# Cross-attention head: where two output chunks and the second group's query chunks are split

## The chip, the cores and the metric

One Trainium2 chip, one core of it. The metric is the device time of one execution in microseconds (us), the median of several runs. Engines are named as the profile names them: PE is TensorE's matmul stream, PEld its weight loads, DVE is VectorE, ACT is ScalarE, POOL is GpSimd, SP is SyncE, which here issues the loads.

## What is computed

Two layers over x (16 sequences of 64 tokens, 512 features: 1024 token rows, 8 tiles of 128): a windowed attention, a gated feed-forward part, a cross-attention and a routed feed-forward part, each on a layer-normed x and each added back to x. The change touches the third:

```
q = (layernorm(x) @ Wq) in 32 heads of 128;  k, v = (ctx @ Wk), (ctx @ Wv) in 8 heads of 128
q, k = rotary(q), rotary(k)
scores = q k^T / sqrt(128), masked;  attn = softmax(scores)
x = x + (attn v) @ Wo
```

Four query heads share one key and value head, so the work falls into 8 groups; a group has 512 columns of Wq, 128 of Wk, 128 of Wv and 512 rows of Wo.

## The kernel before

Every float32 product is made of three matmuls (`mm3`, lines 121 to 123): each operand is split into a high part and a low part. A weight chunk of 128 x 512 is split by two engines: ACT copies the loaded chunk `raw` to the high part (line 1354, `high`), and POOL subtracts it from the chunk, which gives the low part (line 1507, `low`). `W` is a ring that holds both parts.

Cross-attention is a software pipeline of 64 units: unit n treats token tile n % 8 of group n // 8. Each engine has a function `step(n, u, g)`, and its instructions run strictly in the order written there. The first eight units are written out with n a plain number (`past` is false), the later ones stand in a loop. In step n

- PE makes keys and values of unit n (`KV`, weights `ca_wkv`), then the queries of two heads (`QT`, weights `W`, operand `NTh`/`NTl`) as soon as `rope_read` of the unit before is given, transposes K (line 1293), transposes the token tiles that are due (line 233), then does the scores of unit n - 2 (line 1309), the transposes of the probabilities of unit n - 3 (line 1319), the output product of unit n - 4 (`O`) and the value product of unit n - 3 (line 1343).
- DVE, where tiles are due, counts them (line 198), aggregates (208), adds epsilon (210), and normalises (222, `X` to `qT`); then row sums and reciprocals of unit n - 3, the rotary products of unit n (line 1474), then cap and row maxima of unit n - 2 (1490, 1495), and last the low part of the transposed tiles (245).
- POOL raises the variance of the due tiles to the power -1/2 (line 216, `root`, the operand that `normalise` waits for), scales the probabilities of unit n - 3 (line 1534), makes low parts of weights (line 1507), adds the rotary products (lines 1547 and 1550), and subtracts the maxima of unit n - 2 (line 1557).
- ACT does exp of unit n - 3 (1379), high parts of the attention output (1385), copies K and V (1395, 1396), the transposed probabilities (1403), the high parts of due tiles (239) and of weights (1354).

The norm of the eight token tiles is not finished when cross-attention begins: tiles 0 and 1 are made ahead of the pipeline, and units 0, 1 and 2 each make two more (`rows_due`, tiles 2n + 2 and 2n + 3). The work list of the weights in these units is written out by hand: `first_wo_high` and `first_wo_low` treat output chunks of group 0, `weights_high(n, u, g)` and `weights_low(n, u, g)` treat the chunk that is due in unit n, of the next group: query chunks 0 to 3 for n = 0 to 3, then a `ca_wkv` chunk and an output chunk for n = 4 to 7.

The loads come through a ring of two `raw` buffers. SP issues the load of chunk p when the low part of the chunk two places before it is made; it waits on the counter `w_split`, which every low part of a chunk raises by one:

```
sp.wait_ge(S["w_split"], 8 * g + (before - 1))
chunk_loader(sp, g, p)
```

Of the kernel before, what the change touches and what calls it, by code (L numbers as in the profile page):

```python
# [31 lines left out]
EC = E // P  # L32
# [61 lines left out]
def live(n, total):  # L94

    return not isinstance(n, int) or 0 <= n < total
# [1076 lines left out]
def cross_attention(nc, sh, d, norm, next_norm, cross):  # L1173
# [11 lines left out]
    with ExitStack() as st:  # L1185
# [45 lines left out]
        with nc.Block() as block:  # L1231
# [19 lines left out]
            def split_source(n, u, g):  # L1251


                w = (u + AHEAD) % 16
                p, par = w % 8, w // 8
                if p < EC:
                    return [(raw[:, p % 2, :], [x[:, par, p, :] for x in wq],
                             (cross.raw_loaded[p % 2], 64 * g + 16 * (p // 2 + 1)))]
                p -= EC
                return [(kvraw[:, p, :], [x[:, par, p, :] for x in wkv], (cross.kv_loaded, 32 * g + 32)),  # L1260
                        (raw[:, p % 2, :], [x[:, par, p, :] for x in wo],
                         (cross.raw_loaded[p % 2], 64 * g + 32 + 16 * (p // 2 + 1)))]
# [86 lines left out]
            @block.scalar  # L1349
            def _(act):  # L1350
                def high(part):
                    src, dst, loaded = part
                    act.wait_ge(*loaded)
                    return nc.scalar.activation(dst[0], src, ACT.Copy)  # L1354

                def weights_high(n, u, g):
                    if live(n + AHEAD, UNITS + EC):
                        if u % 8 == 0 and (not isinstance(n, int) or n >= 8):
                            act.wait_ge(S["qk_mm"], 8 * g)
                        if u % 8 == 4 and (not isinstance(n, int) or n >= 8):  # L1360
                            act.wait_ge(S["o_mm"], 8 * g)
                        *kv, q_or_o = split_source(n, u, g + 1)
                        if kv:
                            high(kv[0]).then_inc(S["kv_hi"], 1)
                        high(q_or_o).then_inc(S["w_hi"], 1)

                def first_wo_high(chunks):
                    for p in chunks:
                        high(split_source(p - EC, p - EC + 2 * TT, 0)[1]).then_inc(S["w_hi"], 1)

                def step(n, u, g):
                    past = not isinstance(n, int)
                    rows, tiles, banks = rows_due(n)

                    m = n - 3
                    if live(m, UNITS):
                        act.wait_ge(S["subbed"], m + 1)
                        s = sm[:, (u - 3) % 2, :, :]
                        nc.scalar.activation(s, s, ACT.Exp).then_inc(S["exped"], 1)  # L1379

                    m = n - 4
                    if live(m, UNITS):
                        act.wait_ge(S["av_mm"], m + 1)
                        for b2 in range(2):
                            last = nc.scalar.activation(aT[0][:, :, b2 * SEQ:(b2 + 1) * SEQ],
                                                        AV[:, b2, :].rearrange("p (h q) -> p h q", h=GRP), ACT.Copy)
                        last.then_inc(S["av_hi"], 1)

                    if live(n, UNITS):
                        act.wait_ge(S["kv_mm"], n + 1)  # L1390
                        if past or n >= 1:
                            act.wait_ge(S["qk_mm"], n)
                        if past or n >= 4:
                            act.wait_ge(S["av_mm"], n - 3)
                        nc.scalar.activation(K, KV[:, 0:HD], ACT.Copy)
                        nc.scalar.activation(V[:, u % 4, :], KV[:, HD:], ACT.Copy).then_inc(S["kv_copied"], 1)

                    m = n - 3
                    if live(m, UNITS):
                        act.wait_ge(S["pp_mm"], m + 1)  # L1400
                        if past or m >= 1:
                            act.wait_ge(S["av_mm"], m)
                        nc.scalar.activation(pT, PP, ACT.Copy).then_inc(S["pp_copied"], 1)  # L1403
                    for t in tiles:
                        rows.high(act, t, banks[t % 2])
                    if not past and n == 0:
                        first_wo_high(range(2, EC))
                    elif not past and n == 1:
                        weights_high(0, 0, 0)
                        weights_high(1, 1, 0)  # L1410
                    else:
                        weights_high(n, u, g)


                for t in FIRST:
                    for p in (2 * t, 2 * t + 1):
                        high(split_source(p - EC, p - EC + 2 * TT, 0)[0]).then_inc(S["kv_hi"], 1)
                for t in FIRST:
                    norm.high(act, t, rows_due(0)[2][t % 2])
                first_wo_high(range(2))  # L1420
                pipeline(act, step, 0, *STEPS[1:])

            @block.vector
# [78 lines left out]
            def _(gp):  # L1502
# [6 lines left out]
                def weights_low(n, u, g):  # L1509
                    if live(n + AHEAD, UNITS + EC):  # L1510
                        *kv, q_or_o = split_source(n, u, g + 1)
                        if kv:
                            gp.wait_ge(S["kv_hi"], EC * g + (u % EC + EC + 1))
                            low(kv[0]).then_inc(S["kv_split"], 1)
                        gp.wait_ge(S["w_hi"], n + (AHEAD + 1))
                        low(q_or_o).then_inc(S["w_split"], 1)

                def first_wo_low(chunks):
                    for p in chunks:
                        gp.wait_ge(S["w_hi"], EC + p + 1)  # L1520
                        low(split_source(p - EC, p - EC + 2 * TT, 0)[1]).then_inc(S["w_split"], 1)

                def step(n, u, g):
                    past = not isinstance(n, int)
                    j = u % 2
                    rows, tiles, _ = rows_due(n)
                    for tile in tiles:
                        rows.root(gp, tile, tile % 2)

                    m, w = n - 3, (u - 3) % 2  # L1530
                    if live(m, UNITS):
                        gp.wait_ge(S["recip"], m + 1)
                        s = sm[:, w, :, :]
                        nc.gpsimd.tensor_tensor(s, s, rc[:, w, :].unsqueeze(2).broadcast_to([P, 4, SEQ]),  # L1534
                                                ALU.mult).then_inc(S["probs"], 1)
                    if past or n not in range(2):
                        weights_low(n, u, g)

                    if live(n, UNITS):
                        slot = u // 2 % 2  # L1540
                        gp.wait_ge(S["rope_read"], n + 1)
                        if past or n - j > 2:
                            gp.wait_ge(S["sc_mm"], n - (j + 2))
                        if not past and n == 2:
                            gp.wait_ge(norm.transposed, TT + 2)
                        parts = [x[:, 0:2 * PAIR].rearrange("p (m b q) -> p m b q", m=2, b=4) for x in (xc, xs)]
                        last = nc.gpsimd.tensor_tensor(qT[:, slot, j, :, :].rearrange("p b (m q) -> p m b q", m=2),  # L1547
                                                       *parts, ALU.add)
                        if j == 1:
                            last = nc.gpsimd.tensor_tensor(kT[:, slot, :], xc[:, 2 * PAIR:], xs[:, 2 * PAIR:], ALU.add)  # L1550
                        last.then_inc(S["roped"], 1)

                    m, w = n - 2, u % 2
                    if live(m, UNITS):
                        gp.wait_ge(S["maxed"], m + 1)
                        s = sm[:, w, :, :]
                        nc.gpsimd.tensor_tensor(s, s, mx[:, w, :].unsqueeze(2).broadcast_to([P, 4, SEQ]),  # L1557
                                                ALU.subtract).then_inc(S["subbed"], 1)
                    if not past and n == 0:
                        first_wo_low(range(2, EC))  # L1560
                    if not past and n == 1:
                        weights_low(0, 0, 0)
                        weights_low(1, 1, 0)


                def first_kv_low(chunks):
# [490 lines left out]
```

## Time and profile before

| | us |
|---|---|
| median of 3 runs | 1130.06 (1130.03 to 1131.46) |
| the profiled execution, own time | 1132.62 |
| its span in the trace | 1130.8 |
| PE busy in the span | 1045.0 (92%) |
| POOL busy | 514.7 (46%) |
| DVE busy | 661.4 (58%) |

The span is what lies between the first and the last instruction in the trace; the time of that execution holds 1.8 us more around it. Cross-attention runs from about 382 to 990 us of the span. All times of rows are us from the span's start. A timeline row gives start, duration, engine, line, operation, output and input, how many instructions are merged in it, and in brackets the idle time of the engine ahead of it with what ended it.

### The profile page before, as it was taken

What the parts mean: (1) busy time and instruction counts of PE and PEld (TensorE: products, weight loads), DVE (VectorE), ACT (ScalarE), POOL (GpSimd) and SP (SyncE); (2) the same over time, 40 slices, a digit from 0 to 9 for tenths busy, and PEclk for the clock granted to TensorE, in tenths of its full rate; (3) what the DMA queues carried; (4) which work ended last, traced back from release to release, by engine and by line L of the source; (5) the groups of instructions that cost most, each with busy time, mean ns of one, the idle gap of its engine ahead of it and who ended that gap; (6) DMA issues with size and microseconds to landing.
All of it is one profiled execution on the core that took longest, in us unless ns stands there. A gap on an engine that the chain in (4) does not pass through costs nothing. (4 is left out here: it accounts for less than half of the span.)

```text
span 1130.8 us, 24015 instructions
## 1 busy us (share of the span) xinstructions
PE 1045.0 (92%) x9170; PEld 869.1 (77%) x9170; DVE 661.4 (58%) x1357; ACT 352.3 (31%) x826; POOL 514.7 (46%) x594
## 2 busy tenths in 40 slices
PE   6899988999999889999999999999999999745993
PEld 3677777888887678888888888888888888534783
DVE  4799873544544675656555565656555666741324
ACT  3677743222222323222222222222222222211331
POOL 3555531422123365445454454444544442337755
PEclk9899998999999889999999999999999999976997
DMA  7100006656450021111011110011010000036768
GB/s 237 23 3 4 4 4 177 209 192 212 151 205 30 29 72 33 47 29 48 29 33 51 31 46 30 29 48 29 28 57 29 29 10 1 1 129 213 242 215 270
DMA packets 51806, 92.07 MB, mean 81 GB/s; under 512 B 10748, under 2 KB 24316, under 8 KB 51260
## 3 DMA queue, kind: packets, MB, share of 16 engines
q1 hardware_dynamic: 42108, 69.13, 19.4%
q10 hardware_dynamic: 6624, 12.06, 3.1%
q0 software_dynamic: 2976, 9.44, 2.5%
q8 instruction: 76, 1.25, 0.5%
q14 instruction: 22, 0.18, 0.0%
HBM read 77.25 MB, written 36.18 MB: 100 GB/s over the span
## 5 line engine op out<-in xcount | busy, mean ns | idle before, releaser
L121 PE MATMUL PS<-NTh,W 128*128 128x256 f32 (+2 forms) x688 | 217.1, 315 | 0.0
L122 PE MATMUL PS<-NTl,W 128*128 128x256 f32 (+2 forms) x688 | 214.2, 311 | 0.0
L123 PE MATMUL PS<-NTh,W 128*128 128x256 f32 (+2 forms) x688 | 214.2, 311 | 0.0
L122 PEld LDWEIGHTS PS<-NTl,W 128*128 128x128 f32 (+1 forms) x688 | 131.3, 191 | 7.0
L123 PEld LDWEIGHTS PS<-NTh,W 128*128 128x128 f32 (+1 forms) x688 | 129.4, 188 | 8.6
L121 PEld LDWEIGHTS PS<-NTh,W 128*128 128x128 f32 (+1 forms) x688 | 129.6, 188 | 7.2
L1507 POOL TENSOR_TENSOR W<-ca_raw,W 128x512 fp32r<-128x512 f32 x64 | 82.6, 1292 | 109.7 <-ACT W L1354 109.7
L1445 DVE TENSOR_REDUCE ca_su<-room 128x4 f32<-128x256 f32 x64 | 26.8, 419 | 154.0 <-ACT room L1379 154.0
L1474 DVE TENSOR_TENSOR room<-PS,ca_sinT 64x512 f32<-64x512 f32 (+1 forms) x192 | 115.0, 599 | 2.6
L121 PE MATMUL PS<-W,ca_aTh 128*128 128x512 f32 x256 | 106.9, 417 | 3.1 <-DVE X L1462 3.1
L122 PE MATMUL PS<-W,ca_aTh 128*128 128x512 f32 x256 | 101.3, 396 | 0.0
L123 PE MATMUL PS<-W,ca_aTl 128*128 128x512 f32 x256 | 100.9, 394 | 0.0
L1379 ACT ACTIVATE room<-room 128x256 f32<-128x256 f32 x64 | 26.8, 419 | 227.1 <-POOL room L1557 227.1
L1547 POOL TENSOR_TENSOR qT<-room 128x512 f32<-128x512 f32 x64 | 81.7, 1277 | 29.1 <-DVE room L1474 27.7
L1474 DVE TENSOR_TENSOR room<-PS,ca_cosT 128x512 f32<-128x512 f32 (+1 forms) x96 | 57.8, 602 | 56.8 <-PE PS L1293 56.4
L1044 POOL TENSOR_TENSOR ff_hl<-ff_hf,W 128x512 fp32r<-128x512 f32 (+1 forms) x22 | 28.6, 1302 | 132.9 <-ACT W L939 132.9
L1000 DVE TENSOR_TENSOR X<-X,PS 128x512 f32<-128x512 f32 x88 | 60.3, 686 | 48.8 <-PE PS L123 48.3
L1403 ACT ACTIVATE room<-PS 128x256 f32<-128x256 f32 x64 | 24.6, 385 | 186.1 <-PE PS L1319 186.1
L121 PE MATMUL PS<-ca_wkvh,CTh 128*128 128x256 f32 x256 | 79.3, 310 | 2.2 <-issue 2.2
L1534 POOL TENSOR_TENSOR room<-room,ca_rc 128x256 f32<-128x256 f32 x64 | 39.3, 613 | 76.7 <-DVE ca_rc L1447 76.7
L123 PE MATMUL PS<-ca_wkvh,CTl 128*128 128x256 f32 x256 | 72.4, 283 | 0.0
L122 PE MATMUL PS<-ca_wkvl,CTh 128*128 128x256 f32 x256 | 72.1, 282 | 0.0
(253 smaller groups left out, 2354.4 us busy)
## 6 DMA issues: line engine op xcount, KB each, us to landing
ca_raw<-in_L_Wq SPq DMA_DIRECT2D x32, 256.0 KB, 2.8
ca_raw<-in_L_Wo SPq DMA_DIRECT2D x32, 256.0 KB, 2.6
rf_raw<-in_experts SPq DMA_DIRECT2D x28, 256.0 KB, 4.3
room<-slots ACTq DMA_DIRECT2D x23, 256.0 KB, 3.4
outs<-room ACTq DMA_DIRECT2D x23, 256.0 KB, 3.3
outs<-blank SPq DMA_DIRECT2D x11, 512.0 KB, 8.8
room<-in_L_Wg SPq DMA_DIRECT2D x10, 256.0 KB, 2.9
room<-in_L_Wu SPq DMA_DIRECT2D x10, 256.0 KB, 3.1
```

Of the source, the lines that this page charges most:

```text
L121: nc.tensor.matmul(out, l_hi, r_hi, start=first, stop=False)
L122: nc.tensor.matmul(out, l_hi, r_lo, start=False, stop=False)
L123: return nc.tensor.matmul(out, l_lo, r_hi, start=False, stop=last)
L1000: nc.vector.tensor_tensor(sh.X[:, t, :], sh.X[:, t, :], D[:, t % 4, :], ALU.add).then_inc(S["added"], 1)
L1044: nc.gpsimd.tensor_tensor(hl[:w, slot, tok], hf[:w, half, :], hh[:w, slot, tok].bitcast(F32), ALU.subtract).then_inc(S["h_split"], 1)
L1379: nc.scalar.activation(s, s, ACT.Exp).then_inc(S["exped"], 1)
L1403: nc.scalar.activation(pT, PP, ACT.Copy).then_inc(S["pp_copied"], 1)
L1445: nc.vector.reduce_sum(su[:, w, :], sm[:, w, :, :], AX_X).then_inc(S["summed"], 1)
L1474: return nc.vector.tensor_tensor(out[out_rows, some].rearrange("p (m k) -> p m k", m=count), x[rows, :].rearrange("p (m k) -> p m k", m=co ...
L1507: return nc.gpsimd.tensor_tensor(dst[1], src, dst[0].bitcast(F32), ALU.subtract)
L1534: nc.gpsimd.tensor_tensor(s, s, rc[:, w, :].unsqueeze(2).broadcast_to([P, 4, SEQ]), ALU.mult).then_inc(S["probs"], 1)
L1547: last = nc.gpsimd.tensor_tensor(qT[:, slot, j, :, :].rearrange("p b (m q) -> p m b q", m=2), *parts, ALU.add)
```

## The change

The same instructions run, on the same data, in another order on POOL and ACT. What moves, with units counted from 0:

- the low parts of output chunks 2 and 3 of group 0 stood at the end of unit 0 on POOL; they now stand in unit 1, behind its two roots;
- the high and low parts of the next group's query chunks 0 and 1 stood together in unit 1 (ACT and POOL); they now stand together at the end of unit 2, on POOL behind the subtraction of the maxima;
- query chunks 2 and 3 stood in units 2 and 3, one each, on POOL ahead of the rotary additions; they now stand together at the end of unit 3.

```diff
@@ ACT, step @@
                     if not past and n == 0:
                         first_wo_high(range(2, EC))
-                    elif not past and n == 1:
-                        weights_high(0, 0, 0)
-                        weights_high(1, 1, 0)
-                    else:
+                    elif not past and n in (2, 3):
+                        for k in range(2 * n - 4, 2 * n - 2):
+                            weights_high(k, k, 0)
+                    elif past or n != 1:
                         weights_high(n, u, g)
@@ POOL, step @@
                     for tile in tiles:
                         rows.root(gp, tile, tile % 2)
+                    if not past and n == 1:
+                        first_wo_low(range(2, EC))
...
-                    if past or n not in range(2):
+                    if past or n not in range(4):
                         weights_low(n, u, g)
...
-                    if not past and n == 0:
-                        first_wo_low(range(2, EC))
-                    if not past and n == 1:
-                        weights_low(0, 0, 0)
-                        weights_low(1, 1, 0)
+                    if not past and n in (2, 3):
+                        for k in range(2 * n - 4, 2 * n - 2):
+                            weights_low(k, k, 0)
```

POOL, from the rotary addition of unit 0 to that of unit 3, before (`norm_rstd` is the root, `W<-ca_raw,W` a low part of a weight chunk, `qT<-room` and `room<-room` the rotary additions, `ca_mx` the maxima, `ca_rc` the reciprocals):

```order
L1547 TENSOR_TENSOR qT<-room 128x2x4x64
L1507 TENSOR_TENSOR W<-ca_raw,W 128x512 x2
L216 TENSOR_TENSOR norm_rstd<-norm_veps,inverse_root 128x1 x2
L1547 TENSOR_TENSOR qT<-room 128x2x4x64
L1550 TENSOR_TENSOR room<-room 128x256
L1507 TENSOR_TENSOR W<-ca_raw,W 128x512 x2
L216 TENSOR_TENSOR norm_rstd<-norm_veps,inverse_root 128x1 x2
L1507 TENSOR_TENSOR W<-ca_raw,W 128x512
L1547 TENSOR_TENSOR qT<-room 128x2x4x64
L1557 TENSOR_TENSOR room<-room,ca_mx 128x256
L1534 TENSOR_TENSOR room<-room,ca_rc 128x256
```

and the same place of POOL now (the lines below line 1530 have moved down by two), to the scaling of unit 1's probabilities:

```order
L1549 TENSOR_TENSOR qT<-room 128x2x4x64
L216 TENSOR_TENSOR norm_rstd<-norm_veps,inverse_root 128x1 x2
L1507 TENSOR_TENSOR W<-ca_raw,W 128x512 x2
L1549 TENSOR_TENSOR qT<-room 128x2x4x64
L1552 TENSOR_TENSOR room<-room 128x256
L216 TENSOR_TENSOR norm_rstd<-norm_veps,inverse_root 128x1 x2
L1549 TENSOR_TENSOR qT<-room 128x2x4x64
L1559 TENSOR_TENSOR room<-room,ca_mx 128x256
L1507 TENSOR_TENSOR W<-ca_raw,W 128x512 x2
L1536 TENSOR_TENSOR room<-room,ca_rc 128x256
L1549 TENSOR_TENSOR qT<-room 128x2x4x64
L1552 TENSOR_TENSOR room<-room 128x256
```

Both pairs of roots stand directly behind the rotary additions now, the first pair of low parts directly behind the first roots; the other two pairs of low parts stand directly ahead of a scaling of probabilities (the second is the one after these rows).

ACT, from the high parts of tiles 4 and 5 on, before:

```order
L239 ACTIVATE NTh<-PS 128x4x128 x2
L1354 ACTIVATE W<-ca_raw 128x512 x2
L1395 ACTIVATE room<-PS 128x128
L1396 ACTIVATE room<-PS 128x128
L239 ACTIVATE NTh<-PS 128x4x128 x2
L1354 ACTIVATE W<-ca_raw 128x512
L1379 ACT_TABLE_LOAD
```

and now:

```order
L239 ACTIVATE NTh<-PS 128x4x128 x2
L1395 ACTIVATE room<-PS 128x128
L1396 ACTIVATE room<-PS 128x128
L239 ACTIVATE NTh<-PS 128x4x128 x2
L1354 ACTIVATE W<-ca_raw 128x512 x2
L1379 ACT_TABLE_LOAD
```

Unit 1 has no high parts of weights on ACT any more, and two stand ahead of the table load of the first exp, where one stood. PE's and DVE's orders are the same.

## Rows read from the trace of the kernel before

**Rows 1.** Busy time by stretch: span of stretch, PE, PEld, DVE, ACT, POOL, PEclk, DMA.

```profile
408.05:411.50 3.45, 0.94 (x7) 0.78 (x8) 1.57 (x3) 0.28 (x1) 2.39 (x4) 1.00 0.45 137
411.50:414.90 3.40, 3.40 (x18) 3.40 (x17) 2.77 (x6) 2.71 (x4) 1.71 (x2) 0.50 0.06 20
981.50:984.90 3.40, 2.08 (x9) 1.75 (x10) 2.96 (x9) 0.07 (x1) 0.56 (x2) 1.00 0.00 0
984.90:988.30 3.40, 2.61 (x17) 1.59 (x15) 2.17 (x5) 1.66 (x4) 0.61 (x1) 1.00 0.00 0
455.00:890.00 435.00, 432.83 (x3030) 377.79 (x3029) 260.53 (x555) 114.25 (x362) 212.71 (x242) 1.00 0.13 37
```

**Rows 2.** Timeline of PE, units 1 to 4.

```profile
401.01 1.71 PE L233 MATMUL PS<-const,qT 128*128 128x128 f32 x8 [1.91 <-DVE qT L222]
...
404.93 0.36 PE L121 MATMUL PS<-NTh,W 128*128 128x256 f32 x1
...
410.56 1.41 PE L233 MATMUL PS<-const,qT 128*128 128x128 f32 x8 [2.53 <-DVE qT L222]
...
415.54 0.28 PE L121 MATMUL PS<-NTh,W 128*128 128x256 f32 x1
...
419.31 0.39 PE L1319 MATMUL PS<-const,room 128*128 128x128 f32 x2
...
427.11 0.39 PE L1319 MATMUL PS<-const,room 128*128 128x128 f32 x2
```

**Rows 3.** Timeline of POOL, units 0 to 4.

```profile
397.25 2.52 POOL L1507 TENSOR_TENSOR W<-ca_raw,W 128x512 fp32r<-128x512 f32 x2
399.73 1.17 POOL L216 TENSOR_TENSOR norm_rstd<-norm_veps,inverse_root 128x1 f32<-128x1 f32 x2
...
406.11 0.74 POOL L1550 TENSOR_TENSOR room<-room 128x256 f32<-128x256 f32 x1
406.81 2.51 POOL L1507 TENSOR_TENSOR W<-ca_raw,W 128x512 fp32r<-128x512 f32 x2
409.28 1.17 POOL L216 TENSOR_TENSOR norm_rstd<-norm_veps,inverse_root 128x1 f32<-128x1 f32 x2
...
415.67 0.62 POOL L1557 TENSOR_TENSOR room<-room,ca_mx 128x256 f32<-128x256 f32 x1
...
424.10 0.62 POOL L1557 TENSOR_TENSOR room<-room,ca_mx 128x256 f32<-128x256 f32 x1
425.91 0.61 POOL L1534 TENSOR_TENSOR room<-room,ca_rc 128x256 f32<-128x256 f32 x1 [1.20 <-DVE ca_rc L1447]
```

**Rows 4.** Timeline of DVE, units 1 and 2.

```profile
398.55 0.15 DVE L210 TENSOR_SCALAR norm_veps<-norm_mv 128x1 f32<-128x1 f32 x1
...
400.31 1.16 DVE L222 TENSOR_SCALAR qT<-X,norm_mv,norm_rstd 128x512 f32<-128x512 f32 x2 [1.32 <-POOL norm_rstd L216]
401.39 0.68 DVE L1474 TENSOR_TENSOR room<-PS,ca_cosT 128x512 f32<-128x512 f32 x1
...
403.93 0.86 DVE L1474 TENSOR_TENSOR room<-PS,ca_sinT 64x256 f32<-64x256 f32 x2
...
407.41 0.15 DVE L210 TENSOR_SCALAR norm_veps<-norm_mv 128x1 f32<-128x1 f32 x1
...
409.86 1.16 DVE L222 TENSOR_SCALAR qT<-X,norm_mv,norm_rstd 128x512 f32<-128x512 f32 x2 [2.00 <-POOL norm_rstd L216]
```

**Rows 5.** Timelines of DVE, then POOL: a normalisation beside a large POOL instruction.

```profile
60.31 1.24 DVE L222 TENSOR_SCALAR qT<-X,norm_mv,norm_rstd 128x512 f32<-128x512 f32 x1
...
60.21 1.05 POOL L663 TENSOR_TENSOR wa_sm<-wa_sm,wa_mx 128x512 f32<-128x512 f32 x1 [0.78 <-DVE wa_mx L590]
```

**Rows 6.** Line 222, durations of all its instructions (ns, min/median/max).

```profile
L222 DVE TENSOR_SCALAR qT<-X,norm_mv,norm_rstd x20: 536/548/1236, 60.3 to 995.6; 128x512 f32<-128x512 f32 x20
```

**Rows 7.** Timeline of ACT, unit 3.

```profile
416.32 0.42 ACT L1379 ACTIVATE room<-room 128x256 f32<-128x256 f32 x1 [1.91 <-POOL room L1557]
```

**Rows 8.** Tile `ca_raw`, its loads: time from issue to landing.

```profile
DMA to landing us min/median/max: 2.3/2.7/3.5
```

## The prediction

> **What bounds the kernel now.** I read the busy time by stretch first, then the timelines of the head of cross-attention. From 455 to 890 us PE is busy 432.83 of 435 us [rows 1]. The reader should see that from there on cross-attention costs what PE's matmuls cost, so that a change ahead of it moves everything behind by exactly what PE gains or loses before it. The change runs the same instructions and only touches units 0 to 3, so the place to look is where PE still stands idle: 1.91 us ahead of the transposes of tiles 4 and 5 (401.01) and 2.53 us ahead of those of tiles 6 and 7 (410.56) [rows 2]. Both end on DVE's normalisation, and that in turn waited for POOL's root, 1.32 and 2.00 us [rows 4]. Why the roots were late is in POOL's timeline [rows 3]: the root of unit 1 starts at 399.73, when two low parts (397.25 + 2.52) are through, and that of unit 2 at 409.28, again behind two (406.81 + 2.51). The operands were there: epsilon was added by 398.70 and 407.56 [rows 4].
>
> After the second gap there is a second loss. From 411.50 to 414.90 the granted clock is 0.50, that is 1.2 GHz instead of 2.4, and PE is busy all the time; in the stretch before it PE had been busy for 0.94 of 3.45 us only, at full clock [rows 1].
>
> **Part 1: output chunks 2 and 3 go behind the roots of unit 1.** The first root can start at about 398.8 (398.70 and 0.1 us for the handover) instead of 399.73, 0.9 us sooner, and the first normalisation and the transposes of tile 4 with it. The second normalisation is another matter. It reads and writes SBUF beside the low part that POOL now starts at once. A row pair shows such a meeting [rows 5]: POOL's instruction runs from 60.21 to 61.26, DVE's normalisation starts 0.10 us later and takes 1.24 us, to 61.55, where the median one takes 0.55 [rows 6]. So it ends 0.29 us after POOL's instruction has ended. Here: roots end at 398.8 + 1.17 = 399.97, the first low part runs 1.26 us (half of 2.52 [rows 3]) to 401.2, and the second normalisation ends at 401.2 + 0.29 = 401.5. Before, the pair ended at 400.31 + 1.16 = 401.47 [rows 4]. DVE's rotary products, which stand behind it, start at 401.4 either way and end at 403.93 + 0.86 = 404.79 [rows 4], and it is these that release the queries of unit 2 at 404.93 [rows 2]. **Value of part 1: 0.0 us.** The bounds are 0 and 0.9 us; I take the lower one, because the nearest row is the same pair of instructions in the same order, POOL's first.
>
> The Trainium skill (GPSIMD Engine Reference, section Key points) says that GpSimd shares its SBUF interfaces with VectorE, with contention for DVE instructions in a 2-port perf mode or with two SBUF inputs. By that rule alone part 1 is worth 0; without it the sum below would be 0.9 us larger, 3.3 us. The trace agrees with it: 1.24 us beside POOL against 0.55 us. It speaks against this part of the change.
>
> **Part 2: query chunks 0 and 1 leave unit 1.** POOL's rotary additions of unit 1 end at 406.85 [rows 3] as before, and nothing stands ahead of the roots of unit 2 any more. They can start when epsilon is added, at 407.56 + 0.1 = 407.65, instead of 409.28. **1.6 us.** No large POOL instruction follows them (the next waits for the rotary products), so these normalisations keep their 1.16 us [rows 4], and the transposes start at 410.56 - 1.6 = 408.9. PE's idle time ahead of them falls from 2.53 to 0.9 us.
>
> **Part 3: the clock.** With a gap of 0.9 us PE's clock should stay full. Around 982 us PE has gaps too and is busy 2.08 of 3.40 us, and in the next stretch the clock is still 1.00 [rows 1]. The half-clock stretch of 3.40 us, fully busy, would take half as long, 1.7 us less; 0.1 us I take off, since the second normalisation still holds PE up between the transposes of tiles 6 and 7. **1.6 us.** Bounds: 0, if the clock falls all the same, and 1.7. From 410.56 to the queries of unit 3 at 415.54 [rows 2] are 4.98 us; they become 3.4. These queries then start at 408.9 + 3.4 = 412.3, 3.2 us sooner.
>
> **Part 4: what is given back.** The subtraction of unit 0's maxima stood at 415.67 [rows 3]; with the rotary addition of unit 2 no longer behind a low part it comes at about 412.7. It is now followed by two low parts, 2.5 us, to 415.8, and the scaling of unit 0's probabilities comes behind them and ends at 416.4. PE, 3.2 us sooner than 419.31 [rows 2], would want these at 416.1. **Loss 0.3 us**, at a place where the next one is larger and takes it in. ACT has one more high part ahead of its table load; exp stood at 416.32, right behind the subtraction [rows 7], and is now wanted at 413.35. Before, ACT was free at 416.32 - 1.91 = 414.4 [rows 7]; what stands there comes 1.6 us sooner and is 0.6 us longer (the pair of high parts for one), so it is free at 413.4. Cost 0 to 0.1 us, which the loss just named hides.
>
> In unit 3 the subtraction comes at 424.10 - 3.2 = 420.9 and ends at 421.5. Two low parts follow, to 424.0, then the scaling (0.61 [rows 3]) to 424.6, and PE's transposes at 424.7. Before, these started at 427.11 [rows 2], with the scaling at 425.91 in time. So of the 3.2 us **0.8 us are given back** here, and PE is 2.4 us ahead of before. From here PE has no gap: in unit 5 the scaling stands behind its subtraction as before, and I count over 1 us between its end and PE's turn.
>
> Loads: SP issues query chunks 2 and 3 once the low parts of 0 and 1 are made, at 414.5 and 415.8. At 3.5 us, the slowest landing [rows 8], the last is there at 419.3; ACT has made both high parts by 420, and is wanted for exp at 421.5. Cost 0, cover 1.5 us. The first output chunk of the next group is issued when the low part of query chunk 2 is made, at 422.8, and lands at 425.5 by the median [rows 8], about 0.5 us after ACT could use it; the cover in unit 5 takes that in.
>
> **Sum:** 0.0 + 1.6 + 1.6 - 0.8 = 2.4 us less. It is made against the profiled execution, 1132.62 us with a span of 1130.8. That execution is 2.6 us above the median of 1130.06, so the runs without the profiler may lack one half-clock stretch that the trace shows. I take the gain off the median: **1127.7 us**.
>
> **The rivals.** A measurement of this kernel can tell about 0.2%, 2.3 us, from no change.
>
> *A: the forecast.* Gain 2.0 to 2.9 us. Chance 0.45.
>
> *B: the runs compared do not have the half-clock stretch.* Where the clock stays full after the 2.53 us gap, the old kernel reaches unit 4 about 1.3 us sooner (not 1.7, since its scaling then waits for POOL), and the change gains 2.4 - 1.3 = 1.1 us: 1129.0. For it: the runs' 1130.06 against the profiled 1132.62. Against it: the trace has the stretch. Chance 0.27.
>
> *C: no collision in part 1.* If DVE gets hold of the memory first, the second normalisation keeps its 0.55 us, all of unit 1 comes 0.9 us sooner, and the gain is 3.3: 1126.8. For it: only 0.1 us lies between the two starts. Against it: the pair of [rows 5]. Chance 0.10.
>
> *D: nothing that counts.* The clock still falls in unit 2, since gaps of about 1 us in unit 1 lie close ahead of the one of 0.9 us, and the low parts ahead of the scalings take 0.8 us of the 1.6: 1129.3. For it: no row has such gaps so close together. Against it: the row at 984.90. Chance 0.12.
>
> *E: slower.* The new gap in unit 4, 0.5 us ahead of the transpose of K and 0.8 us ahead of the probabilities' transposes, makes the clock fall there, while it falls in unit 2 as before: -0.8 + 1.7 = 0.9 us slower, 1131.0. It decides from the point where gaps of 0.5 and 0.8 us cost the clock; the fall in these rows has 2.53 us of idle time ahead of it [rows 1, 2], and the row at 984.90 shows the clock kept at 2.08 of 3.40 us busy. To be slower by over 0.2% the loads of part 4 would have to be late besides, by several us. Chance 0.06.
>
> **How the numbers follow.** Over 0.2% faster: 0.27 of A's 0.45 (the gain lies hardly above the bound), C's 0.10, 0.02 of B: 0.39. Within 0.2%: 0.18 of A, 0.25 of B, 0.12 of D, 0.03 of E: 0.58. Slower by over 0.2%: 0.03. The range reaches from C with half a us for the runs' own spread, 1126.3, to B and D with the same, 1129.9; E and the far tail are left out.
>
> **What would show it.** In the changed kernel's trace: roots of unit 1 at 398.8 and of unit 2 at 407.7; the first normalisation of unit 1 at 0.55 us, the second at about 1.5; rotary products of unit 1 again at 401.4; transposes of tiles 6 and 7 at 408.9 after a gap of 0.9 us; full clock from there; queries of unit 3 at 412.2; the probabilities' transposes of unit 4 at 424.7 behind a POOL scaling that stands behind two low parts. The prediction is wrong if the second normalisation takes 0.55 us (C), if the granted clock is 0.50 around 412 us (D), or if ACT's exp of unit 4 waits for a high part whose load is late.

## The result, and the profile after

The changed kernel takes 1129.61 us (median of 22 runs, 1127.30 to 1132.02) against 1132.30 us for the kernel before (median of 22 runs, 1126.96 to 1135.65). The ratio is 0.9978, 95% interval 0.9968 to 0.9988: 2.5 us less, between 1.4 and 3.6 (the two medians alone differ by 2.7). The first three runs of the kernel before, 1130.06 us in the middle, were on the fast side of what it does: the median of its 22 runs is 2.2 us higher.

The profiled execution of the changed kernel has a span of 1126.3 us, 4.5 us less than before, which is more than the change is worth. So the traces are compared stretch by stretch. As a **yardstick** for the changed place I take the time from the start of PE's transpose of K in unit 1 to the start of its transposes of the probabilities in unit 4. Ahead of it PE's work is the same in both kernels. Behind it little is left to gain or lose: from its end to the last transpose of K in cross-attention lie between 531.2 and 531.9 us in all twelve traces of this study. It ends on the last row of [rows 2], and in the kernel before it starts on this row of PE's timeline (columns as there: start, duration, engine, line, what; in brackets the idle time ahead):

```profile
398.83 0.27 PE L1293 MATMUL PS<-const,room 128*128 128x128 f32 x1
```

427.11 - 398.83 = 28.28 us. PE's timeline of the changed kernel, units 1 to 4:

```profile
400.16 0.27 PE L1293 MATMUL PS<-const,room 128*128 128x128 f32 x1
401.31 0.63 PE L233 MATMUL PS<-const,qT 128*128 128x128 f32 x4 [0.88 <-DVE qT L222]
402.76 0.63 PE L233 MATMUL PS<-const,qT 128*128 128x128 f32 x4 [0.82 <-DVE qT L222]
...
406.07 0.55 PE L121 MATMUL PS<-NTh,W 128*128 128x256 f32 x1 [0.29 <-DVE room L1474]
...
410.07 1.25 PE L233 MATMUL PS<-const,qT 128*128 128x128 f32 x8 [0.51 <-DVE qT L222]
...
413.46 0.28 PE L121 MATMUL PS<-NTh,W 128*128 128x256 f32 x1
...
417.59 0.44 PE L1319 MATMUL PS<-const,room 128*128 128x128 f32 x2 [0.19 <-POOL room L1536]
...
425.74 0.44 PE L1319 MATMUL PS<-const,room 128*128 128x128 f32 x2 [0.54 <-POOL room L1536]
```

The yardstick is 425.74 - 400.16 = 25.58 us, 2.70 us less. Read from its start, the steps stand against [rows 2] as follows:

| us behind the transpose of K in unit 1 | before | changed | difference |
|---|---|---|---|
| first transposes of unit 1 | 2.18 | 1.15 | -1.03 |
| queries of unit 2 | 6.10 | 5.91 | -0.19 |
| transposes of unit 2 | 11.73 | 9.91 | -1.82 |
| queries of unit 3 | 16.71 | 13.30 | -3.41 |
| probabilities' transposes, unit 3 | 20.48 | 17.43 | -3.05 |
| probabilities' transposes, unit 4 | 28.28 | 25.58 | -2.70 |

The first row gains a us and the second gives 0.8 of it back. The reason is in DVE's timeline, to be read against [rows 4]:

```profile
399.80 0.15 DVE L210 TENSOR_SCALAR norm_veps<-norm_mv 128x1 f32<-128x1 f32 x1
...
400.62 2.00 DVE L222 TENSOR_SCALAR qT<-X,norm_mv,norm_rstd 128x512 f32<-128x512 f32 x2 [0.37 <-POOL norm_rstd L216]
402.54 0.68 DVE L1474 TENSOR_TENSOR room<-PS,ca_cosT 128x512 f32<-128x512 f32 x1
...
409.38 1.16 DVE L222 TENSOR_SCALAR qT<-X,norm_mv,norm_rstd 128x512 f32<-128x512 f32 x2 [0.36 <-POOL norm_rstd L216]
```

and POOL's, against [rows 3]:

```profile
400.03 1.17 POOL L216 TENSOR_TENSOR norm_rstd<-norm_veps,inverse_root 128x1 f32<-128x1 f32 x2 [1.49 <-DVE norm_veps L210]
401.06 2.69 POOL L1507 TENSOR_TENSOR W<-ca_raw,W 128x512 fp32r<-128x512 f32 x2
...
408.79 1.17 POOL L216 TENSOR_TENSOR norm_rstd<-norm_veps,inverse_root 128x1 f32<-128x1 f32 x2 [0.81 <-DVE norm_veps L210]
...
413.87 0.61 POOL L1559 TENSOR_TENSOR room<-room,ca_mx 128x256 f32<-128x256 f32 x1
414.44 2.52 POOL L1507 TENSOR_TENSOR W<-ca_raw,W 128x512 fp32r<-128x512 f32 x2
416.92 0.61 POOL L1536 TENSOR_TENSOR room<-room,ca_rc 128x256 f32<-128x256 f32 x1
...
422.02 0.62 POOL L1559 TENSOR_TENSOR room<-room,ca_mx 128x256 f32<-128x256 f32 x1
422.59 2.52 POOL L1507 TENSOR_TENSOR W<-ca_raw,W 128x512 fp32r<-128x512 f32 x2
425.07 0.62 POOL L1536 TENSOR_TENSOR room<-room,ca_rc 128x256 f32<-128x256 f32 x1
```

The second normalisation of unit 1 and the first low part, each by itself:

```profile
401.24 1.38 DVE L222 TENSOR_SCALAR qT<-X,norm_mv,norm_rstd 128x512 f32<-128x512 f32 x1
...
401.06 1.27 POOL L1507 TENSOR_TENSOR W<-ca_raw,W 128x512 fp32r<-128x512 f32 x1
```

The pair of normalisations takes 2.00 us in unit 1 and 1.16 us in unit 2: only the first pair has a low part of POOL's beside it. The low part ends at 402.33, the second normalisation 0.29 us behind it, at 402.62. DVE's wait for the roots falls from 1.32 and 2.00 us to 0.37 and 0.36. Both scalings (L1536) now stand directly behind two low parts, and PE waits for both of them. The granted clock, in the busy time by stretch (columns as in [rows 1]), is full behind the gap of unit 2:

```profile
403.50:406.90 3.40, 3.11 (x16) 2.84 (x15) 3.31 (x7) 0.97 (x3) 1.14 (x2) 0.50 0.77 205
406.90:410.30 3.40, 2.89 (x25) 2.69 (x25) 2.90 (x9) 0.00 (x0) 2.25 (x4) 1.00 0.34 102
410.30:413.70 3.40, 3.40 (x31) 3.20 (x29) 3.31 (x7) 2.93 (x5) 1.08 (x1) 1.00 0.02 5
424.00:430.00 6.00, 5.43 (x31) 4.15 (x32) 3.31 (x7) 1.21 (x3) 4.70 (x5) 1.00 0.29 90
455.00:890.00 435.00, 433.10 (x3033) 377.51 (x3031) 261.10 (x556) 113.55 (x360) 213.36 (x242) 1.00 0.13 37
```

It is half earlier, from 403.5 to 406.9, behind the two gaps of unit 1 (0.88 and 0.82 us). There it costs next to nothing. The keys and values of unit 2 run in it, behind which PE has to wait for DVE's rotary products anyway, and so do the first queries of unit 2; what these lose comes off the gap behind them, 0.51 us, where a second trace of this kernel (experiment 7), without half clock there, has 0.81. The kernel before has such a stretch too, from 401.3 to 404.7, behind its gap of 1.91 us. ACT's timeline of unit 3 shows the loads that come late for its two high parts (0.36 and 0.68 us of waiting), and the 1.92 us of idle time between them and exp, which take the delay in:

```profile
418.81 0.63 ACT L1354 ACTIVATE W<-ca_raw 128x512 fp32r<-128x512 f32 x1 [0.36 <-DMA ca_raw<-in_L_Wq]
420.12 0.63 ACT L1354 ACTIVATE W<-ca_raw 128x512 fp32r<-128x512 f32 x1 [0.68 <-DMA ca_raw<-in_L_Wq]
422.68 0.42 ACT L1379 ACTIVATE room<-room 128x256 f32<-128x256 f32 x1 [1.92 <-POOL room L1559]
```

What is left of the 4.5 us: the yardstick gives 2.7, but the changed execution had 1.33 us more ahead of it (400.16 against 398.83). Of these 0.38 us stand there already at the first transposes of cross-attention (385.58 against 385.20); behind them the granted clock stays at half until 393.2 us, in the kernel before only until 391.0. And the stretch from the last transpose of K in cross-attention (958.99 before, 957.28 now) to the end of the span is 169.0 us instead of 171.8; the remaining 0.3 us lie between. No instruction of that last stretch is changed. Over the twelve traces it lies between 168.3 and 173.6 us whatever stands in the head. In the three traces of the changed kernel it makes 3.5 us of the 4.1 us by which their spans differ; of the executions without a trace nothing is shown.

### The profile page after: what moved, and what is told of

Same layout as the page of the kernel before. It is cut to its first block and busy times, and to the rows that moved or that the text cites. A ratio compares the mean times of both kernels' runs of the same rounds, so it can differ in the third digit from the quotient of the medians.

```text
span 1126.3 us, 24015 instructions
## 1 busy us (share of the span) xinstructions
PE 1044.5 (93%) x9170; PEld 866.7 (77%) x9170; DVE 661.8 (59%) x1357; ACT 352.6 (31%) x826; POOL 515.1 (46%) x594
## 5 line engine op out<-in xcount | busy, mean ns | idle before, releaser
L1536 POOL TENSOR_TENSOR room<-room,ca_rc 128x256 f32<-128x256 f32 x64 | 39.3, 614 | 74.4 <-DVE ca_rc L1447 74.4
```

## The experiments

All are judged first by the yardstick, and then by the ratio to the kernel before, whose interval is 1.1 to 1.9 us to either side. The yardstick came back within 0.1 us wherever a kernel was traced again (25.58, 25.66 and 25.58 us for the changed kernel), except for the kernel before, where it depends on the clock (experiment 7). Between kernels that differ by a us or less, intervals of this width decide nothing.

**1. Only the low parts of output chunks 2 and 3 moved.** The edit, on the kernel before:

```diff
+                    if not past and n == 1:
+                        first_wo_low(range(2, EC))
...
-                    if not past and n == 0:
-                        first_wo_low(range(2, EC))
```

> The kernel before with only the low parts of output chunks 2 and 3 moved, from the end of unit 0 to behind the roots of unit 1; the query chunks stay in units 1 to 3. Yardstick in each trace: from the start of PE's transpose of K in unit 1 to the start of its probabilities' transposes in unit 4, 28.3 us in the kernel before and 25.6 in the changed one. Theory 1 (the sooner roots are lost again, because POOL's low part slows the second normalisation): roots of unit 1 sooner, the pair of normalisations about 2.0 us instead of 1.16, queries of unit 2 within 0.2 us of before, yardstick 28.1 to 28.3, time within 0.3 us of before. Theory 2 (the roots of unit 1 carry the gain): queries of unit 2 0.9 us sooner, yardstick 27.3 or less, time 0.9 us or more below before.

PE's timeline of this kernel:

```profile
397.89 0.27 PE L1293 MATMUL PS<-const,room 128*128 128x128 f32 x1
399.13 0.63 PE L233 MATMUL PS<-const,qT 128*128 128x128 f32 x4 [0.97 <-DVE qT L222]
...
409.52 1.40 PE L233 MATMUL PS<-const,qT 128*128 128x128 f32 x8 [2.54 <-DVE qT L222]
...
426.07 0.39 PE L1319 MATMUL PS<-const,room 128*128 128x128 f32 x2
```

and DVE's:

```profile
398.44 2.00 DVE L222 TENSOR_SCALAR qT<-X,norm_mv,norm_rstd 128x512 f32<-128x512 f32 x2 [0.37 <-POOL norm_rstd L216]
...
408.83 1.16 DVE L222 TENSOR_SCALAR qT<-X,norm_mv,norm_rstd 128x512 f32<-128x512 f32 x2 [2.01 <-POOL norm_rstd L216]
```

The yardstick is 28.18 us, 0.10 less than before; ratio 1.0009 (0.9997 to 1.0021). The gap of 2.5 us in unit 2 stands untouched, and the granted clock falls behind it as before. Theory 2 falls: the sooner roots of unit 1 are worth nothing in this form.

**2. Only the query chunks moved.** The changed kernel with this put back:

```diff
-                    if not past and n == 1:
-                        first_wo_low(range(2, EC))
...
+                    if not past and n == 0:
+                        first_wo_low(range(2, EC))
```

> The changed kernel with output chunks 2 and 3 put back to the end of unit 0; only the query chunks are moved, in pairs, to units 2 and 3. Theory 1: the whole gain is here: the pair of normalisations in unit 1 is 1.16 us again, roots of unit 2 free of low parts, yardstick 25.5 to 25.8, time like the changed kernel's, about 2.5 us below before. Theory 2: a third of the gain or more is missing, yardstick 26.5 or more.

PE's timeline:

```profile
398.56 0.27 PE L1293 MATMUL PS<-const,room 128*128 128x128 f32 x1
400.73 1.25 PE L233 MATMUL PS<-const,qT 128*128 128x128 f32 x8 [1.90 <-DVE qT L222]
...
408.66 1.24 PE L233 MATMUL PS<-const,qT 128*128 128x128 f32 x8 [0.51 <-DVE qT L222]
...
424.33 0.44 PE L1319 MATMUL PS<-const,room 128*128 128x128 f32 x2 [0.54 <-POOL room L1534]
```

25.77 us, ratio 0.9979 (0.9963 to 0.9996). The gap of unit 1 is back at 1.90 us, and all but 0.2 us of the gain is there. The two halves add up: -0.10 and -2.51 against -2.70.

**3. POOL waits for the second normalisation.** On the changed kernel:

```diff
                     if not past and n == 1:
+                        gp.wait_ge(rows.normed, tiles[-1] + 1)
                         first_wo_low(range(2, EC))
```

> The changed kernel, where POOL in unit 1 waits until the second normalisation is done before it begins the low parts of output chunks 2 and 3. Theory 1: the second normalisation takes 0.55 us instead of 1.45, the rotary products of unit 1, the queries of unit 2 and all behind them come 0.9 us sooner than in the changed kernel, yardstick 24.7, time 0.9 us below the changed one. Rival (the second normalisation is slow for another reason, or something else holds unit 2): yardstick 25.6 or more, since POOL's low parts now begin later.

DVE's timeline:

```profile
400.79 1.16 DVE L222 TENSOR_SCALAR qT<-X,norm_mv,norm_rstd 128x512 f32<-128x512 f32 x2 [0.37 <-POOL norm_rstd L216]
```

and PE's:

```profile
400.25 0.27 PE L1293 MATMUL PS<-const,room 128*128 128x128 f32 x1
401.48 1.25 PE L233 MATMUL PS<-const,qT 128*128 128x128 f32 x8 [0.96 <-DVE qT L222]
...
424.99 0.44 PE L1319 MATMUL PS<-const,room 128*128 128x128 f32 x2 [0.54 <-POOL room L1537]
```

The pair takes 1.16 us, and the yardstick is 24.74 us, 0.84 us less than in the changed kernel, although the low parts begin 0.9 us later. That is the collision, taken away by itself. The time shows nothing of it, 0.9978 (0.9965 to 0.9992), which an interval of this width allows; this trace also has the longest stretch behind cross-attention, 173.6 us.

**4. The pairs of low parts split around the scaling.** On the changed kernel, without the wait of experiment 3:

```diff
+                    if not past and n in (3, 4):
+                        weights_low(2 * n - 5, 2 * n - 5, 0)
                     if past or n not in range(4):
...
                     if not past and n in (2, 3):
-                        for k in range(2 * n - 4, 2 * n - 2):
-                            weights_low(k, k, 0)
+                        weights_low(2 * n - 4, 2 * n - 4, 0)
```

> The changed kernel with only the split of the query chunks' pairs (one low part behind the subtraction, the other behind the next scaling); POOL does not wait in unit 1. Theory 1: the second normalisation takes 1.45 us as in the changed kernel, the scalings wait for one low part at most, yardstick 24.9 (25.6 less the 0.7 us that ACT's copy leaves of the 0.8), time 0.7 us below the changed one. Rival (the scalings are not what PE waits for in unit 4): 25.6.

From PE's timeline:

```profile
398.19 0.27 PE L1293 MATMUL PS<-const,room 128*128 128x128 f32 x1
...
422.14 0.33 PE L1293 MATMUL PS<-const,room 128*128 128x128 f32 x1 [0.92 <-ACT room L1396]
...
423.15 0.39 PE L1319 MATMUL PS<-const,room 128*128 128x128 f32 x2
```

24.96 us, 0.62 less than the changed kernel; ratio 0.9973 (0.9957 to 0.9989). Nothing stands in brackets at the last row: PE no longer waits for POOL there. What is left is the wait for ACT's copy, 0.92 us ahead of the transpose of K. So the two low parts ahead of each scaling cost the changed kernel 0.6 us.

**5. Wait and split together**, the two diffs above, run twice.

> As the kernel with POOL's wait in unit 1, and besides each pair of query chunks' low parts is split: one behind the subtraction of the maxima (units 2 and 3), the other behind the scaling of the next unit (3 and 4), so that POOL's 1.2 us between subtraction and scaling holds one low part and the scaling waits for none. Theory 1: the 0.3 us and the 0.8 us that the changed kernel gives back at the two scalings are cut to the wait for ACT's copy, yardstick 24.0, time 1.6 us below the changed kernel, 4 us below before. Rival (another wait, ACT's or a load's, takes the place): yardstick 24.7, as without the split.

> The kernel with POOL's wait in unit 1 and the split pairs, once more, beside the changed kernel on one chip. Theory 1: yardstick 24.1 again, and 1.5 us below the changed kernel run beside it, about 0.9965 of before. Rival (what is gained in the head is lost again behind it): yardstick 24.1, but the last transposes of K in cross-attention not 1.5 us nearer to the first than in the changed kernel, and the same time as that.

Yardstick 24.14 and 24.04 us, 1.4 to 1.5 us less than the changed kernel. Ratios 0.9975 (0.9963 to 0.9988) and 0.9971 (0.9959 to 0.9982). Beside the second of them ran the changed kernel:

> The changed kernel a third time, as the partner of the run with wait and split: 0.998 of before within 0.001, yardstick 25.6.

Its yardstick is 25.58 us and its ratio 0.9980 (0.9966 to 0.9994). The last transpose of K stands 557.38 us behind that of unit 1 in the changed kernel (957.67 - 400.29) and 555.88 us in the other (955.08 - 399.20): the 1.5 us last to the end of cross-attention, and the rival falls there. In the time only 1.0 us of difference shows, with intervals that overlap. The ratios put the version 2.8 and 3.3 us below the kernel before, where 4 us were expected. It is likely the fastest of all, but against the changed kernel that is shown by the traces, not by the measured time.

**6. The clock by itself.** On the kernel before, PE is kept busy in the gap:

```diff
                         if n == UNITS:
                             pe.wait_ge(S["rope_read"], UNITS)
+                        if n == 2:
+                            stay_busy(nc, sh.PS[:, 3, :], ident, sh.X[:, 0, :], 2)
```

> The kernel before with two matmuls of no use (the first tile of x times the identity, into a PSUM bank that is free there) on PE in unit 2, ahead of the transposes that wait for the normalisation. PE waits as long as before, but is busy in about 1.7 of the 2.5 us. Theory 1 (1.3 us of the gain is the clock): full clock behind the gap, transposes of unit 2 at the same place, queries of unit 3 about 1.6 us sooner, yardstick 27.0 instead of 28.3, time 1 to 1.3 us below before. Rival (the half-clock stretch does not come from the gap): clock 0.50 as before, yardstick 28.3.

PE's timeline:

```profile
398.45 0.27 PE L1293 MATMUL PS<-const,room 128*128 128x128 f32 x1
...
410.11 1.24 PE L233 MATMUL PS<-const,qT 128*128 128x128 f32 x8 [0.84 <-DVE qT L222]
...
413.50 0.28 PE L121 MATMUL PS<-NTh,W 128*128 128x256 f32 x1
...
425.36 0.39 PE L1321 MATMUL PS<-const,room 128*128 128x128 f32 x2
```

and its busy time by stretch:

```profile
410.70:414.10 3.40, 3.40 (x31) 3.40 (x31) 3.31 (x7) 3.00 (x4) 1.51 (x2) 1.00 0.14 51
```

The transposes of unit 2 stand 11.66 us behind the start of the yardstick, as before (11.73), but the queries of unit 3 at 15.05 instead of 16.71. From the transposes to the queries are 3.39 us instead of 4.98: 1.59 us from the clock alone. At the end of the yardstick 1.37 us of it is left, 26.91 against 28.28. The ratio, 0.9995 (0.9982 to 1.0009), does not show it. The next experiment says why that was to be expected. It also says that this trace gives the price of the half-clock stretch, and no proof that the filling kept the clock up: it can stay full without it.

**7. Both kernels once more, unchanged.**

> The kernel before, unchanged, as a measure of the comparison itself and of how often the half-clock stretch of unit 2 comes. Ratio 1.000 within 0.001. If the stretch follows from the 2.5 us gap alone: again half clock within 2 us behind it, yardstick 28.3. If it depends on when the gap falls (rival B of the prediction): in some executions full clock and 27.0.

> The changed kernel, unchanged, once more: ratio to before 0.998 within 0.001, yardstick 25.6 within 0.2, full clock in units 3 and 4 again.

The kernel before gave 0.9998 (0.9985 to 1.0011) against itself, the changed one 0.9974 (0.9962 to 0.9986) with a yardstick of 25.66 us. The third trace of the changed kernel, above, has 25.58 us. The trace of the kernel before is the interesting one. PE's timeline:

```profile
399.82 0.27 PE L1293 MATMUL PS<-const,room 128*128 128x128 f32 x1
...
411.47 1.24 PE L233 MATMUL PS<-const,qT 128*128 128x128 f32 x8 [2.16 <-DVE qT L222]
...
426.71 0.39 PE L1319 MATMUL PS<-const,room 128*128 128x128 f32 x2
```

and its busy time by stretch:

```profile
410.00:413.40 3.40, 1.93 (x17) 1.76 (x17) 2.52 (x5) 1.25 (x3) 1.36 (x3) 1.00 0.52 159
413.40:416.80 3.40, 3.40 (x31) 3.40 (x31) 2.59 (x5) 1.75 (x2) 2.86 (x3) 1.00 0.15 16
```

The same program, the same wait of 2.00 us on DVE, a gap of over 2 us on PE, and no half clock behind it. (The gap is 0.37 us shorter than in the first trace, since PE came to it later: the half-clock stretch of unit 1 runs from 403.2 to 406.6 here and takes in the first queries of unit 2. The transposes stand 11.65 us behind the start all the same.) The yardstick is 26.89 us, like that with the gap filled (26.91). So rival B of the prediction is real in some executions: of the three traces with this gap and nothing in it, the first one of the kernel before and that of experiment 1 have the half-clock stretch, and this one does not.

## Why the prediction held

It gave 1127.7 us in a range of 1126.3 to 1129.9; 1129.61 was measured. The forecast of a gain was 2.4 us, and 2.5 (1.4 to 3.6) was measured. The absolute number is 1.9 us too low because it was taken off 1130.06 us, the median of three runs, and 22 runs put the kernel before at 1132.30. That error, 2.2 us, is as large as the way from 1127.7 to the upper end of the range; that the time still lies 0.3 us inside is luck. The gain of 2.5 us agrees with the forecast of 2.4 more closely than an interval of 2.2 us can test; the traces test it better. The same three runs were the prediction's argument for rival B (runs that lack the half-clock stretch which the trace shows). As an argument it falls, though the rival itself turned out real: the 22 runs lie at the profiled 1132.62 us.

- **Part 1, 0.0 us.** Right, and shown by experiments 1 and 3. The second normalisation ended 0.29 us behind the low part, as worked out from the one meeting in [rows 5], and took 1.38 us, where the prediction said about 1.5; the first transposes came a us sooner, the queries of unit 2 only 0.2. Here the rule of the Trainium skill on the SBUF interfaces that GpSimd and VectorE share (GPSIMD Engine Reference, Key points) and the trace agree: 1.38 us with a low part beside it, 0.55 without, and 0.84 us of yardstick between the two. Which of the rule's conditions this instruction meets, no row shows.
- **Part 2, 1.6 us.** Right: 1.82 us at the transposes of unit 2, of which 0.2 came with the queries; experiment 2, without part 1, has 1.63 (408.66 - 398.56 = 10.10 against 11.73).
- **Part 3, the clock, 1.6 us.** Right in size: 3.41 - 1.82 = 1.59 us between the transposes of unit 2 and the queries of unit 3, and the same 1.59 in experiment 6, where the orders of all other engines are those of before. The prediction held it against an execution that has the stretch; in those that do not, the kernel before is 1.39 us better (28.28 - 26.89), and the gain is 26.89 - 25.58 = 1.3 us, where rival B said 1.1.
- **Part 4, 0.8 us given back.** The difference falls from 3.41 to 2.70 us, so 0.7: 0.36 at the first scaling, 0.35 more at the second. The prediction had 0.3 and 0.8 for the two, the first taken in by the second. The loads were as counted: ACT finished its high parts at 420.75 and was wanted at 422.68, a cover of 1.9 us where 1.5 was said.
- **Rivals.** C (no collision) fell: in all five traces with this order (the changed kernel three times, experiments 1 and 4) the pair takes 2.00 us. D fell: there is no half clock behind the transposes of unit 2 in any of the eight traces of kernels that have the query chunks moved. What it feared of the gaps of unit 1 did come, in two of the three traces of the changed kernel, but further ahead, where DVE holds PE up anyway. E fell: the gaps ahead of the transposes of unit 4 cost no clock (1.00 from 424 to 430 us), and no load was late enough to reach PE.

What stays open is how often the kernel before has the half-clock stretch. The measured 2.5 us (1.4 to 3.6) fits nearly any mixture of 2.7 us with it and 1.3 without, and the share was not counted. So the parts are shown for an execution with the stretch, and how they make up the measured median is not.

## What to carry to other kernels

Where a small instruction that two engines wait for stands behind large ones, look at who runs beside the large ones once they are moved: a low part directly behind the roots took from DVE what the sooner root had given, and one wait on a semaphore gave it back. Large work of a helper engine belongs into the time in which that engine waits for a round trip of others (here 1.2 us between subtraction and scaling, room for one low part, not for two). And when a change is worth 0.2%, compare stretches between two fixed instructions of the trace; the runs of one kernel spread by about 4 to 9 us here, and the traces differ by up to 5.3 us in a stretch that the change does not touch.

## What the runs showed of the hardware

**The same program does not always lose the clock at the same place.** After 2.53 and 2.54 us of idle time (the kernel before, experiment 1) PE ran at half clock for 3.4 us; after 2.16 us in experiment 7 it stayed at full clock. In unit 1 a gap of 1.91 us (the kernel before), 1.90 (experiment 2) and 1.83 (experiment 7) was followed by half clock, and one of 1.82 us (experiment 6) was not. Two gaps of 0.96 and 0.82 us close together were followed by half clock in the third trace of the changed kernel and not in its second; its first, with 0.88 and 0.82, had half clock too. So the length of the gap alone does not decide. What does was not tried.

**DVE's normalisation, begun 0.1 to 0.2 us after a large POOL instruction, ended 0.29 us after it.** Beside 1.05 us of POOL it took 1.24 us [rows 5], beside the low part of 1.27 us 1.38 us, and 0.55 us alone. These are the two lengths that were seen. POOL, which began first, lost nothing in that low part: 1.27 us, where the two of experiment 3, which wait until the normalisation is done, take 1.29 us each. Its second low part took 1.46 us; it began 0.33 us before the normalisation ended, and then ran beside DVE's rotary products. Which of them slowed it is not shown.
